# Softmax attention over 2304 tokens: queries and keys as two float32r terms in 50 rows in place of three bfloat16 terms in 99 rows

## The reference

```python
q = jnp.einsum('bnc,dc->bnd', xf, Wq) + q_bias
k = jnp.einsum('bnc,dc->bnd', xf, Wk)
v = jnp.einsum('bnc,dc->bnd', xf, Wv) + v_bias
...
q = q * cos + _rotate_half(q) * sin
k = k * cos + _rotate_half(k) * sin
scale = hd ** (-0.5)
attn = jnp.einsum('bhnd,bhmd->bhnm', q * scale, k)
attn = jax.nn.softmax(attn, axis=-1)
out = jnp.einsum('bhnm,bhmd->bhnd', attn, v)
```

## Time and profile before

| what | value |
|---|---|
| time, median of 3 runs | 7288.85 us (7287.42 to 7288.94) |
| the profiled execution, its own time | 7286.52 us |
| its span, first to last instruction | 7285.0 us |
| mean granted clock of TensorE | 0.908 |
| PE busy in the span | 6277.0 us, 86% |
| PEld | 4258.7 us, 58% |
| DVE | 4851.3 us, 67% |
| ACT | 3258.3 us, 45% |
| POOL | 2365.2 us, 32% |
| `rope_projections` | 0 to 291 us of the span |
| `softmax_heads` | 291 to 2200 us of the span |

### The profile page before, as it was taken

One profiled execution on the slowest core, in us unless ns is written; L12 is line 12 of the kernel. 1 busy time (PEld: TensorE's weight loads), 2 busy tenths in 40 slices (PEclk: granted clock), 3 DMA queues, 4 the chain that ended last, 5 costly groups with the idle time before them and its releaser, 6 DMA issues. The chain is left out here.

```text
span 7285.0 us, 235159 instructions
## 1 busy us (share of the span) xinstructions
PE 6277.0 (86%) x87979; PEld 4258.7 (58%) x87979; DVE 4851.3 (67%) x8094; ACT 3258.3 (45%) x5652; POOL 2365.2 (32%) x2687
## 2 busy tenths in 40 slices
PE   6799999999995686799999960897799999999977
PEld 4366666666664553587787860565455555555546
DVE  5798889888963301454554553113789999999976
ACT  2177777777781142233333310122444444444432
POOL 0011111121111000000000013002299999999951
PEclk7699999999997787899999955998999999999976
DMA  3211111111115314101100041324811111111133
GB/s 116 84 40 42 40 40 41 40 41 45 44 30 136 99 41 134 51 1 30 30 1 21 1 135 37 76 71 125 244 48 37 37 37 37 38 38 37 36 78 95
DMA packets 424935, 428.71 MB, mean 59 GB/s; under 512 B 77729, under 2 KB 397961, under 8 KB 419051
## 3 DMA queue, kind: packets, MB, share of 16 engines
q1 hardware_dynamic: 342123, 339.77, 16.8%
q0 software_dynamic: 62528, 59.16, 3.5%
q10 hardware_dynamic: 19712, 21.53, 0.9%
HBM read 253.62 MB, written 166.55 MB: 58 GB/s over the span
## 5 line engine op out<-in xcount | busy, mean ns | idle before, releaser
L653 DVE TENSOR_REDUCE softmax_part_max<-softmax_ring 128x1 f32<-128x512 f32 (+1 forms) x2880 | 1624.3, 630 | 223.1 <-PE softmax_ring L560 165.4
L2577 POOL TENSOR_TENSOR retention_decayed<-retention_third,retention_decay_table 128x384 f32<-128x384 f32 x1728 | 1690.4, 1006 | 107.9 <-ACT retention_third L2599 103.9
L2558 DVE TENSOR_TENSOR retention_decayed<-retention_scores,retention_decay_table 128x768 f32<-128x768 f32 x1728 | 1655.2, 958 | 90.6 <-PE retention_scores L2519 59.4
L689 ACT ACTIVATE softmax_probs<-softmax_scores 128x768 f32<-128x768 f32 x1728 | 1392.3, 811 | 380.2 <-PE softmax_scores L584 266.9
L2599 ACT COPY retention_third<-retention_scores 128x384 f32<-128x384 f32 x1728 | 826.5, 478 | 893.2 <-PE retention_scores L2519 893.2
L2519 PE MATMUL retention_scores<-retention_q_half,retention_k_piece 96*32 96x384 bf16 x20736 | 1183.4, 326 | 37.2 <-DMA retention_v_piece<-ret_v 29.7
L2531 PE MATMUL retention_sums<-retention_decayed,retention_v_piece 128*32 128x288 f32 x13824 | 1181.3, 407 | 3.1 <-POOL retention_decayed L2577 0.6
L560 PE MATMUL softmax_ring<-softmax_k_next,softmax_q_next 96*32 96x512 bf16 (+1 forms) x11520 | 1114.6, 371 | 45.7 <-DMA softmax_k_next<-rope_k 31.6
L584 PE MATMUL softmax_scores<-softmax_q_third,softmax_k_piece 99*32 99x384 bf16 x13824 | 891.3, 329 | 61.3 <-DMA softmax_q_third<-maxima 28.6
L2519 PEld LDWEIGHTS retention_scores<-retention_q_half,retention_k_piece 96*32 96x32 bf16 x20736 | 623.2, 95 | 523.4 <-DVE retention_decayed L2558 43.3
L595 PE MATMUL softmax_sums<-softmax_probs,softmax_v_piece 128*32 128x192 f32 x13824 | 886.7, 328 | 11.7 <-ACT softmax_result L670 6.0
(11 more groups left out here) (318 smaller groups left out, 7929.9 us busy)
## 6 DMA issues: line engine op xcount, KB each, us to landing
ret_v<-ret_proj_values SPq DMA_DIRECT2D x8, 1728.0 KB, 8.5
retention_v_piece<-ret_v SPq DMA_DIRECT2D x144, 96.0 KB
softmax_q_third<-rope_q SPq DMA_DIRECT2D x192, 54.0 KB
softmax_q_next<-rope_q POOLq DMA_DIRECT2D x64, 162.0 KB, 4.1
softmax_k_piece<-rope_k SPq DMA_DIRECT2D x192, 54.0 KB
softmax_k_next<-rope_k POOLq DMA_DIRECT2D x64, 162.0 KB, 6.9
ret_q<-ret_proj_parts SPq DMA_DIRECT2D x48, 216.0 KB, 2.9
ret_k<-ret_proj_parts SPq DMA_DIRECT2D x48, 216.0 KB, 3.1
```

Source lines behind the costliest of these rows:

```text
L653: nc.vector.reduce_max(part_max[:, j, c:c + 1], ring[m % DEEP][:, 0:CHUNKS[c][1]], axis=X)\
L689: nc.scalar.activation(probs[n % 4][:, :].rearrange("p (c q) -> p c q", c=2), scores[n % 2][:, :, 0:QC], ACT.Exp, scale=scale).then_inc(ex ...
L2558: nc.vector.tensor_tensor(weights[n % 4][:, 0:2 * QC].rearrange("p (c q) -> p c q", c=2), scores[n % 2][:, 0:2, 0:QC], table[:, table_at(n ...
L2577: nc.gpsimd.tensor_tensor(weights[n % 4][:, 2 * QC:HALF], third[n % 3][:, :], table[:, at:at + QC], ALU.mult)\
```

## The change

Queries and keys are kept as two float32r terms, a rounded one and the rest, in place of three bfloat16 ones. Four pairs of terms make K = 4 x 12 = 48 rows, with two rows for the maxima 50. These rows are held twice in SBUF, at rows 0 and at rows 64 (`ROW`), so that a matmul takes a 64 x 128 tile of the array in its upper or in its lower half, with all 128 columns. A score's two halves c stand in the two halves of the rows, one instruction each; maximum chunk m stands in half m % 2, one instruction. The value matmuls keep their four instructions of 128 x 32.

One set of buffers (`q_rows`, `k_rows`, `values`, three deep) serves both maxima and scores. SP loads a head with nine DMAs behind one wait (for the last value group of the head three before), and sends the maxima as soon as they are made. GpSimd loads nothing; it fills 32 or 18 rows of 2304 elements with -1 in each half of the three key buffers, and SP waits for these six fills before the first load. ScalarE makes the rounded term of the maxima with a second copy, GpSimd the rest with one subtraction. In the order of TensorE, the chunks of a step stand together between score and value. LONG is 6. In `rope_projections` VectorE makes one cast and one subtraction, SP stores with two DMAs.

The diff, without the lines that only rename:

```diff
-        parts = [sb(f"parts{i}", [D, 2, 3, W], BF16) for i in range(2)]
+        parts = [sb(f"parts{i}", [D, 2, 2, W], F32R) for i in range(2)]
...
-                sp.dma_start(q_parts[b, 0:3, :, chunk].rearrange("s p n -> p s n"), parts[c % 2][:, 0, :, :]).then_inc(done, 16)
-                sp.dma_start(q_parts[b, 3:5, :, chunk].rearrange("s p n -> p s n"), parts[c % 2][:, 0, 0:2, :]).then_inc(done, 16)
-                sp.dma_start(k_parts[b, :, :, chunk].rearrange("s p n -> p s n"), parts[c % 2][:, 1, :, :]).then_inc(done, 16)
+                for r, to in enumerate((q_parts, k_parts)):
+                    sp.dma_start(to[b, :, :, chunk].rearrange("s p n -> p s n"), parts[c % 2][:, r, :, :].bitcast(F32)).then_inc(done, 16)
...
-                split_terms(nc, dve, [parts[c % 2][:, :, n, :] for n in range(3)], value, turned_part[:, :, :])\
+                nc.vector.tensor_copy(parts[c % 2][:, :, 0, :], value)
+                dve.drain()
+                nc.vector.tensor_tensor(parts[c % 2][:, :, 1, :], value, parts[c % 2][:, :, 0, :].bitcast(F32), ALU.subtract)\
                     .then_inc(split_done, 1)
...
-    K = sum(n for _, n in q_runs) * d
-    RUNS = len(q_runs)
+    heads = q_terms.shape[2] // d
+    K = 4 * d
+    ROW = 64
...
-    PIECES = 3
-    PT = TILES // PIECES
+    BUFS = 3
+    LOADS = 9
...
-    LONG = 10
+    LONG = 6
     with ExitStack() as ctx:
         sb, ps, sem = allocators(nc, ctx, "softmax")
-        q_third = [sb(f"q_third{i}", [K + 3, THIRD], BF16) for i in range(3)]
-        k_piece = [sb(f"k_piece{i}", [K + 3, PT * P], BF16) for i in range(PIECES)]
-        v_piece = [sb(f"v_piece{i}", [P, PT, 32], F32) for i in range(PIECES)]
-        q_next = [sb(f"q_next{i}", [K, N], BF16) for i in range(2)]
-        k_next = [sb(f"k_next{i}", [K, N], BF16) for i in range(2)]
+        q_rows = [sb(f"q_rows{i}", [ROW + K + 2, N], F32R) for i in range(BUFS)]
+        k_rows = [sb(f"k_rows{i}", [ROW + K + 2, N], F32R) for i in range(BUFS)]
+        values = [sb(f"values{i}", [P, TILES, 32], F32) for i in range(BUFS)]
...
-        max_terms = sb("max_terms", [TILES, 3, P], BF16)
+        tops = sb("tops", [TILES, P], F32)
+        max_terms = sb("max_terms", [TILES, 2, P], F32R)
...
+            def load_head(h, i):
+                at = bass.ds(h % heads * d, d)
+                for r in range(2):
+                    for half in range(2):
+                        rows = slice(r * ROW + half * 2 * d, r * ROW + (half + 1) * 2 * d)
+                        sp.dma_start(q_rows[i][rows, :].bitcast(F32), q_terms[h // heads, half, at, :].unsqueeze(0).to_broadcast([2, d, N]))                          .then_inc(head_in[i], 16)
+                        sp.dma_start(k_rows[i][rows, :].bitcast(F32), k_terms[h // heads, :, at, :]).then_inc(head_in[i], 16)
+                sp.dma_start(values[i][:, :, :], v_rows[h, :, :, :]).then_inc(head_in[i], 16)
...
-            for i in range(3):
-                load_q(0, i)
-                load_kv(0, i)
+                for r in range(2):
+                    at = r * ROW + K
+                    sp.dma_start(q_rows[i][at:at + 2, :].bitcast(F32), m_rows[h, :, :]).then_inc(maxes_in, 16)
+            def head(h, i, following):
+                if following:
+                    maxes_to_rows(h + 1)
+                    load_maxes(h + 1, (i + 1) % BUFS)
+                if following >= BUFS:
+                    sp.wait_ge(valued, (h + 1) * STEPS)
+                    load_head(h + BUFS, i)
...
+            sp.wait_ge(ones_set, 2 * BUFS)
+            load_head(0, 0)
+            sp.dma_start(identity[:, :], ident).then_inc(ident_in, 16)
+            for i in range(1, BUFS):
+                load_head(i, i)
...
-            with sp.Fori(0, n_heads - 1) as h:
-                for i in range(2):
-                    sp.wait_ge(scored, h * STEPS + (i + 1) * TILES)
-                    load_q(h + 1, i)
-                for i in range(PIECES - 1):
-                    sp.wait_ge(valued, h * STEPS + 2 * TILES + (i + 1) * PT)
-                    load_kv(h + 1, i)
-                    if i == 0:
-                        maxes_to_rows(h + 1)
-                        for third in range(2):
-                            load_maxes(h + 1, third)
-                sp.wait_ge(scored, (h + 1) * STEPS)
-                load_q(h + 1, 2)
-                load_maxes(h + 1, 2)
-                sp.wait_ge(valued, (h + 1) * STEPS)
-                load_kv(h + 1, PIECES - 1)
+            load_maxes(0, 0)
+            ROUNDS = (n_heads - BUFS) // BUFS
+            with sp.Fori(0, ROUNDS) as trip:
+                for i in range(BUFS):
+                    head(trip * BUFS + i, i, BUFS)
...
-            for i in range(PIECES):
-                pool.memset(k_piece[i][K:K + 3, :], -1.0).then_inc(ones_set, 1)
-            pool.memset(one[:, :], 1.0).then_inc(ones_set, 1)
-            pool.wait_ge(ones_set, PIECES + 1)
+            for i in range(BUFS):
+                for r in range(2):
+                    at = r * ROW + 32
+                    pool.memset(k_rows[i][at:at + 32 - 14 * r, :].bitcast(F32), -1.0).then_inc(ones_set, 1)
+            pool.wait_ge(ones_set, 2 * BUFS)
...
-                pool.wait_ge(maxes_out, h * 16)
-                nc.gpsimd.tensor_tensor(max_terms[:, 0, :], tops[:, :], one[:, :], ALU.mult).then_inc(term_made, 1)
-                pool.wait_ge(term_made, h * 3 + 1)
-                nc.gpsimd.tensor_tensor(rest[:, :], tops[:, :], max_terms[:, 0, :], ALU.subtract).then_inc(term_made, 1)
-                pool.wait_ge(term_made, h * 3 + 2)
-                nc.gpsimd.tensor_tensor(max_terms[:, 1, :], rest[:, :], one[:, :], ALU.mult).then_inc(term_made, 1)
-                pool.wait_ge(term_made, h * 3 + 3)
-                nc.gpsimd.tensor_tensor(max_terms[:, 2, :], rest[:, :], max_terms[:, 1, :], ALU.subtract)\
+                nc.gpsimd.tensor_tensor(max_terms[:, 1, :].bitcast(F32), tops[:, :], max_terms[:, 0, :].bitcast(F32), ALU.subtract)\
                   .then_inc(terms_ready, 1)
...
+                rows = slice(m % 2 * ROW, m % 2 * ROW + K)
...
-                for g in range(4):
-                    rows = j * P + 32 * g
-                    last = nc.tensor.matmul(ring[m % DEEP][32 * g:32 * g + 32, 0:width], q_next[i][:, rows:rows + 32],
-                                            k_next[i][:, at:at + width], start=True, stop=True)
-                last.then_inc(ring_full, 1)
+                nc.tensor.matmul(ring[m % DEEP][:, 0:width], q_rows[i][rows, j * P:(j + 1) * P], k_rows[i][rows, at:at + width],
+                                 start=True, stop=True).then_inc(ring_full, 1)
...
                 for c in range(2):
-                    for g in range(4):
-                        at = t % PT * P + 32 * g
-                        last = nc.tensor.matmul(scores[n % 2][32 * g:32 * g + 32, c, 0:QC], k_piece[t // PT][:, at:at + 32],
-                                                q_third[third][:, c * QC:(c + 1) * QC], start=True, stop=True)
+                    rows, at = slice(c * ROW, c * ROW + K + 2), third * THIRD + c * QC
+                    last = nc.tensor.matmul(scores[n % 2][:, c, 0:QC], k_rows[i][rows, t * P:(t + 1) * P],
+                                            q_rows[i][rows, at:at + QC], start=True, stop=True)
...
                 for g in range(4):
-                    last = nc.tensor.matmul(sums[32 * g:32 * g + 32, 0:VC], v_piece[t // PT][:, t % PT, :],
+                    last = nc.tensor.matmul(sums[32 * g:32 * g + 32, 0:VC], values[i][:, t, :],
...
+                    share = AHEAD + (MAXES - AHEAD) * (n + 1) // TURN if n < TURN else MAXES + AHEAD * (n + 1 - TURN) // (STEPS - TURN)
...
-                        score(h, n, last_head=not following)
+                        score(h, now, n, last_head=not following)
+                    maxima(n)
                     if n == TOP_STEP and following:
                         turn_top(h + 1)
-                    maxima(2 * n)
                     if n >= 2:
-                        value(h, n - 2)
-                    maxima(2 * n + 1)
...
-                act.wait_ge(terms_ready, h)
-                nc.scalar.copy(tops[:, :], turned_top).then_inc(top_copied, 1)
+                act.wait_ge(maxes_out, h * 16)
+                nc.scalar.copy(tops[:, :], turned_top)
+                nc.scalar.copy(max_terms[:, 0, :], turned_top).then_inc(top_copied, 1)
...
-    q_parts, k_parts = scratch("rope_q", (images, 5, D, N), BF16), scratch("rope_k", (images, 3, D, N), BF16)
-    v_rows, maxima = scratch("rope_v", (images * heads, P, N // P, 32)), scratch("maxima", (images * heads, 3, N), BF16)
+    q_terms, k_terms = scratch("rope_q", (images, 2, D, N)), scratch("rope_k", (images, 2, D, N))
+    v_rows, maxima = scratch("rope_v", (images * heads, P, N // P, 32)), scratch("maxima", (images * heads, 2, N))
```

(47 more changed lines are left out.)

65 lines of the change are left out of this document (16 added, 49 removed).

## The result

The changed kernel takes **8649.6 us** (median of 4 runs, 8630.5 to 8659.0) against 7288.1 us before: a ratio of 1.1879, 95% interval 1.1861 to 1.1898. It is 19% slower. The forecast was slower, at 8310 us; the time lies 30 us above the end of the range (7290 to 8620). The profiled execution has a span of 8628.9 us, 1343.9 more than before.

A forecast was written before the change was run, and what follows sets the result against it. TensorE's stream was taken as the bound inside a head. From 7286.5 us, +998 for 30.7 heads mostly at the lower clock, -20 rope, +11 start and +34 tail gave about 8310 us; range 7290 to 8620.

The forecast's parts named there:

- lower level: Likeliest case: granted clock about 0.5 over most of the softmax stage; 1.73 us a step, 93.6 a head; chance 0.57.
- changes of form: TensorE switching between 64x128 and 128x32 tiles and back in each step: 0.32 us together, bounds 0.18 and 0.36.
- upper level: Rival: the clock comes up and stays; 1.06 us a step, 58.5 a head, 7309 us; chance 0.20.
- Nine tenths: Share of the softmax stage at the lower clock, 93.6 us a head; one tenth at 58.5; together +998 us.
- the gaps: Two drains in each TensorE step, a fifth of 1.73 us as gap; nothing brings the clock up within a head.
- Rope and start: Rope stage: one cast and one subtraction fewer per chunk, -20 us; start: SP waits for six fills, +11 us.
- Tail: 69 steps without chunks after the last transpose, 1.30 us each at the lower clock: +34 us.
- Border: Between heads: TensorE's 1.98 us wait for the maxima goes, since SP sends them as soon as made.
- SP's new wait: SP waits for a head's last value group before nine loads and the next maxima; claimed that nobody waits.

The follow-up runs named there:

- run 1: Changed kernel with 60 extra value-like matmul groups once, without gaps, between the first score and the first step: 8523.7 us.
- run 5: Changed kernel with the value groups of two steps put together behind every second step, rows unchanged: 8222.2 us, median of four executions.
- Run 3: Changed kernel with value product in 64x128 tiles, one in each half, two ring banks in place of three; sums not the value product: 7394.6 us.
- run 4: Changed kernel with each half of the array filled with zeros to 62 rows for a chunk and 64 for a score: 7474.5 us.
- run 6: Changed kernel with full rows, paired value groups and spread chunks: 7388.1 us; also with longer ScalarE loops and an earlier start: 7351.9 us.
- run 2: Changed kernel with two extra value-like groups behind each value group, all but every eighteenth: 8419.1 us.

## Why the prediction was right, and where it was not

- *Direction and mechanism: right; the time was not.* The clock stayed at its lower level, and changes of form ate the gain of the shorter streams. At the upper level a step was forecast at 1.06 us and a head at 58.5; run 1 measured 1.10 and 60.4.
- *The step that failed is the price of the changes of form at the lower clock.* I carried 0.32 to 0.36 us over from the upper level, read from the wide stage. Streams at the lower level are 0.32, 0.43 and 0.64; the measured distances 0.49, 0.56 and 0.79 leave 0.17 + 0.13 + 0.15 = 0.45, and run 5 finds the same 0.45 once in two steps. At the upper level the same changes took 0.36 on average (run 1), so they cost more at the lower level, though not twice as much. A step is 1.84, not 1.73, and a head 100.4, not 93.6: +6.8 x 30.7 = 209 us.
- *"Nine tenths" was wrong.* No head ran at the upper level; there was no reason in any row for the tenth that I kept. It is worth 0.1 x (93.6 - 58.5) x 30.7 = 108 us. These two terms are 317 of the 321 us by which the profiled execution exceeds the likeliest time. The upper end of the range, 99 us a head, stood for 0.44 a step, above the 0.36 that I had named as the bound, and was still too low: 8620 is 10 us below the profiled execution and 30 below the median.
- *Why the clock stayed low: half right.* I named the gaps. Run 3 shows that the changes of form count, but run 4 that the rows do too: 14 unused rows in each half, which I had not weighed, decided between the rivals "upper level" and "lower level". The Trainium skill, "TensorE: Matmul & The Clock Gate", section "Why this matters for your kernels", asks for continuous matmuls without long idle gaps. By that the clock should have come up, with TensorE 99% busy in the profile; the trace speaks against it, with a granted clock of 0.50.
- *Tiling.* The Trainium skill, "TensorEngine Tiling (Array Packing)", section "Tiling Modes", says that a change of tiling mode drains the engine. The trace agrees, for 64x128 and 128x32: the two changes of a step take 0.36 us in run 1 and 0.45 in the changed kernel.
- *Rope and start: two errors that cancel.* The rope stage gave 45 us, not half of 38. VectorE's busy time there fell by the 36 us forecast (186.99 to 150.96), and the stage by still more; its mean granted clock also rose, from 0.77 to 0.85, which no run takes apart. The start cost 34, not 11: the fills took 12.3 us, 12.5 forecast, but behind them 38 us passed until the first head's loads had landed, and the prediction had priced the fills alone. Net -11, forecast -9: the agreement is luck.
- *Tail:* +42, forecast +34; a step there took 1.42 us in place of 1.30, by the same price of the changes of form.
- *Border:* right. After the first score no wait for maxima is left, and SP's new wait held nobody up, at that pace. In run 6, with a head of 60 us, the loads behind it do come late.

## What to carry to other kernels

A matmul form that makes each stream shorter need not make a kernel faster: price the changes of form between neighbouring instructions, at the clock at which they will run, and ask whether what is left still brings the clock up. Where TensorE sits at 1.2 GHz although it seems busy throughout, look at how many rows of the array its tiles fill and how often the form changes: here fourteen rows of zeros in each half brought the changed kernel from about 8631 to 7474 us. Before a large rewrite, take the small waits: sending one transfer earlier and a loop that turns half as often made the kernel before 0.5% faster, and no form of the change did as well.

## What the runs showed of the hardware that I had not expected

Zeros in unused rows of a 64-row tile raised the granted clock from 0.50 to 0.95 (run 4), with durations at equal clock unchanged. Extra matmuls made a kernel faster (run 2, 8419 against 8631). The upper clock, once reached, was kept by steps that did not reach it themselves, until one wait of 4.28 us (run 1). The two changes of form of a step cost more at the lower clock, 0.45 us for 0.36.
